# Decay steps on a ring of three banks, with the pairs on either side run among the steps

## What is computed

```
proj = h @ W_in.T;  gate, h_BC, dt = split(proj)          # 4096, 4096+2*128, 64 columns
h_BC = silu(conv over 4 taps of h_BC)                      # hidden, B, C
dt = softplus(dt + dt_bias);  At = -exp(A_log) * dt        # 64 heads, chunks of 32 tokens
L = exp(segment sums of At within a chunk)                 # [head, chunk, 32, 32]
y = ((C B^T * L) @ (hidden*dt) + chunk states) + D*hidden
x = x + ga * ((rmsnorm(y * silu(gate)) * norm_w) @ W_out.T)
```

## Time and profile before

| | us |
|---|---|
| median of 3 runs | 1593.89 |
| lowest and highest | 1591.78, 1598.0 |
| the profiled execution: its own time | 1599.31 |
| its span, first to last instruction | 1597.2 |
| mean granted TensorE clock | 0.949 of full |
| a transition, from yt of pair 31 to yt of the next batch's pair 0: three of them | 39.38, 40.16, 41.57 |
| the first batch's steps on DVE | 48.16 to 64.38 |

### The profile page before, as it was taken

How to read it: one execution, slowest core, us unless ns; L and a number is a source line. 1 busy time by engine, 2 the same in 40 slices (tenths; PEclk the granted TensorE clock), 3 DMA queues, 4 the chain that set the end, 5 groups by cost and what they waited for, 6 DMA issues and landing times.

```text
span 1597.2 us, 29712 instructions
## 1 busy us (share of the span) xinstructions
PE 1466.8 (92%) x9736; PEld 1143.2 (72%) x9736; DVE 1269.4 (79%) x2138; ACT 966.6 (61%) x1729; POOL 654.2 (41%) x554
## 2 busy tenths in 40 slices
PE   6799999799999789999879999877699999999979
PEld 5666666666766666666576676545598998998979
DVE  2788888698899788989779889943568988998954
ACT  3665666566566566656375656542267888887840
POOL 0134344133447524435814344834024544454530
PEclk7899999999999999999999999977769999999989
DMA  5376567466667755667847667713168989998858
GB/s 189 130 220 218 195 209 242 130 227 209 214 220 249 231 184 195 222 207 240 265 139 232 219 204 233 253 39 108 38 185 282 298 288 300 297 299 276 255 195 268
DMA packets 239686, 343.55 MB, mean 215 GB/s; under 512 B 20761, under 2 KB 191399, under 8 KB 238512
## 3 DMA queue, kind: packets, MB, share of 16 engines
q1 hardware_dynamic: 226096, 299.48, 59.4%
q0 software_dynamic: 13440, 42.19, 7.3%
HBM read 177.65 MB, written 172.30 MB: 219 GB/s over the span
## 4 chain that ended last, share of the span: by engine, by line
PE 64%; DVE 16%; issue 7%; ACT 5%; SPq 3%; DMA 2%; another core or an unknown queue 2%; POOL 1%; DVEq 0%; ACTq 0%; POOLq 0%
PE bank L451 12%; PE bank L618 11%; PE bank L453 10%; PE bank L452 10%; PE bank L629 6%; DVE e L1144 4%; PE bank L817 3%; PE bank L605 3%; DVE m L1185 2%; PE bank L793 2%; ACT e L880 2%; PE bank L763 2%; DVE e L1181 1%; DVE ew_lo L1077 1%
## 5 line engine op out<-in xcount | busy, mean ns | idle before, releaser
L1542 POOL TENSOR_TENSOR ssq<-ssq,ysq 128x512 f32<-128x512 f32 x128 | 167.8, 1311 | 428.7 <-ACT ysq L951 427.2
L1144 DVE SCALAR_TENSOR_TENSOR e<-bank,scal,e 128x511 f32<-128x511 f32 (+2 forms) x384 | 286.2, 745 | 35.2 <-ACT e L946 26.2
L1625 POOL DMA_INDIRECT outputs<-hsw,x_rows x160 | 181.6, 1135 | 238.0 <-DVE hsw L1488 185.7
L451 PE MATMUL bank<-h_hi,wi_hi 128*128 128x512 f32 x512 | 229.8, 449 | 33.2 <-issue 15.1
L618 PE MATMUL bank<-e,wn 128*128 128x512 f32 x512 | 247.6, 607 | 12.3 <-DVE e L1181 12.3
L1529 POOL TENSOR_TENSOR wi_lo<-wi,wi_hi 128x512 fp32r<-128x512 f32 x128 | 164.8, 1288 | 107.8 <-ACT wi_hi L828 107.8
L452 PE MATMUL bank<-h_lo,wi_hi 128*128 128x512 f32 x512 | 206.5, 403 | 0.0
L453 PE MATMUL bank<-h_hi,wi_lo 128*128 128x512 f32 x512 | 206.4, 403 | 0.0
L946 ACT ACTIVATE e<-bank,scal 128x512 f32<-128x512 f32 x128 | 99.4, 777 | 165.0 <-PE bank L453 163.4
L959 ACT ACTIVATE e<-e 128x512 f32<-128x512 f32 x128 | 80.7, 630 | 170.6 <-DVE e L1144 170.0
L1077 DVE TENSOR_TENSOR ew_lo<-ew,ew_hi 128x864 fp32r<-128x864 f32 x160 | 168.5, 1053 | 14.8 <-ACT ew_hi L828 8.1
(11 more groups left out here) (232 smaller groups left out, 3444.5 us busy)
## 6 DMA issues: line engine op xcount, KB each, us to landing
grouped<-zeros_out SPq DMA_DIRECT2D x256, 520.0 KB
ew<-expert_w SPq DMA_DIRECT2D x160, 432.0 KB
wi<-in_w SPq DMA_DIRECT2D x128, 256.0 KB
x_rows<-grouped SPq DMA_DIRECT2D x160, 130.0 KB
wo<-out_w SPq DMA_DIRECT2D x128, 128.0 KB
got<-outputs SPq DMA_DIRECT2D x16, 768.0 KB, 4.3
seg_wb<-seg_const POOLq DMA_DIRECT2D x4, 2048.0 KB, 8.3
seg_wa<-seg_const POOLq DMA_DIRECT2D x4, 2048.0 KB
```

The costliest lines, as they stand in the source:

```text
L451: mm(out, w_hi, x_hi, start=first, stop=False)
L1144: v.scalar_tensor_tensor(dst[:, d:], src[:, 0:SEQ - d], taps(TAPS - 1 - d), dst[:, d:], ALU.mult, ALU.add).then_inc(S[done], 1)
L1542: g_.tensor_tensor(ssq[:, :], ssq[:, :], ysq[:, :], ALU.add).then_inc(S["ssq_done"], 1)
L1625: g_.indirect_dma_start(outputs, bass.IndirectOffsetOnAxis(x_rows[:, i % XD, EMB:EMB + 1].bitcast(U32), 0), y_rows[:, i % YD, :], None, bo ...
```

## The change

1. The steps use a ring of three: banks 6, 2 and 3, and three buffers laid over `m` (two halves) and `xt` (`seg_e`). PE and ACT wait for the step three back in place of eight. PE waits before step 1 for the last `xt`, before step 2 for the last `y_skip`, and ACT before steps 0 to 2 for the last small matmuls (`ssm`).
2. Slot 33 of the old batch (output product, square of y) runs among the next batch's steps: at step 3 on PE and ACT, ahead of step 0 on DVE as before.
3. Sums of squares at step 5, their reading on DVE at step 8, copy out of p_out at step 6.
4. The next batch's pair 0: weights taken in during slot 31 of the old batch, hidden product at step 6, first tap at step 8, taps on DVE at step 10, gate product at step 10. Pair 1's weights are rounded at step 13 and its hidden product runs at step 26. C B^T runs at step 14, its mask at step 18. Both silus of pair 0 stay behind step 31.
5. Batch 0: its pair 0's weights are taken in at step 3; C B^T, its silu and its mask stay behind step 31; PE now waits before step 0 for all 6 taps of B and C (before, ahead of step 6).
6. SP loads the next batch's first two pairs in the loop's last two rounds; POOL starts the second half of the constants behind slot 31 and waits for three of the four send counters.

```diff
-SEG_BANKS = (6, 0, 1, 2, 3, 7, 4, 5)
+SEG_RING, SEG_BANKS = 3, (6, 2, 3)
+SEG_OUT, SEG_SUMS, SEG_HID, SEG_GATHER, SEG_TAP0, SEG_SQUARE, SEG_TAPS, SEG_GATE = 3, 5, 6, 6, 8, 8, 10, 10
+SEG_NEXT_IN, SEG_G, SEG_MASK, SEG_NEXT_HID = 13, 14, 18, 26
...
+            seg_e = (m[:, 0:2, :, :].rearrange("p t h l -> p (t h l)"), m[:, 2:4, :, :].rearrange("p t h l -> p (t h l)"),
+                     xt[:, :, :].rearrange("p t l -> p (t l)"))
...
-                if u >= RING:
-                    pe.wait_ge(S["seg_exp"], n - RING + 1)
+                if u == 1:
+                    pe.wait_ge(S["xt_done"], START["xt_done"] + b * PAIRS)
+                if u == 2:
+                    pe.wait_ge(S["y_skip"], START["y_skip"] + b * PAIRS)
+                if u >= SEG_RING:
+                    pe.wait_ge(S["seg_exp"], n - SEG_RING + 1)
...
+                pe.wait_ge(S["bc_taps"], 2 * (TAPS - 1) * (b + 1))
...
                 for u in range(CHUNK):
+                    if u == SEG_OUT and b:
+                        slot(b - 1, PAIRS + 1, 1, do_hid=False, do_in=False, do_mid=False, do_out="last")
+                        beside(b - 1, PAIRS + 1)
+                    if u == SEG_SUMS and b:
+                        pe.wait_ge(S["xhat"], (BATCH if b == 1 else BATCH + b - 1) * KE)
+                        square_sums(b - 1)
+                    if u == SEG_HID:
+                        hidden(b, 0, 0)
+                    if u == SEG_GATE:
+                        gating(b, 0, 0)
+                    if u == SEG_G and b:
+                        state_products(b)
+                    if u == SEG_NEXT_HID:
+                        hidden(b, 1, 1)
+                    segment(b, u)
+                if b == 0:
+                    state_products(b)
                 beside(b, 0)
-                slot(b, 1, 1, do_out="")
+                pe.wait_ge(S["seg_exp"], (b + 1) * CHUNK)
+                slot(b, 1, 1, do_hid=False, do_out="")
...
# ACT
-                if u >= RING:
-                    act.wait_ge(S["seg_done"], n - RING + 1)
+                if u >= SEG_RING:
+                    act.wait_ge(S["seg_done"], n - SEG_RING + 1)
+                else:
+                    act.wait_ge(S["ssm"], START["ssm"] + b * PAIRS)
...
+                    if u == SEG_OUT:
+                        if b:
+                            slot(b - 1, PAIRS + 1, 1, do_tap=False, do_in=False, next_in=False, take_out=False)
+                            beside(b - 1, PAIRS + 1)
+                        else:
+                            take_in(b, 0, 0)
+                    if u == SEG_GATHER and b:
+                        gather_out(b - 1)
+                    if u == SEG_TAP0:
+                        first_tap(b, 0, 0)
+                    if u == SEG_NEXT_IN:
+                        take_in(b, 1, 1)
                     segment(b, u)
...
# DVE
-                    if u == 5 and b:
+                    if u == SEG_SQUARE and b:
                         mean_square(b - 1)
+                    if u == SEG_TAPS:
+                        slot(b, 0, 0, do_mid=False, finish=False)
+                    if u == SEG_MASK and b:
+                        mask(b)
                     segment(b, u)
...
# POOL
-                    for t in range(HD):
+                    for t in range(3):
                         pool.wait_ge(S[f"sent{t}"], 16 * TOP_K * max(0, b - 1))
...
-                    slot(b, j, j % 2, next_in=j < PAIRS - 1, finish=j > 1)
+                    slot(b, j, j % 2, next_in=j < PAIRS - 1 or j == PAIRS - 1 and b + 1 < BATCH, finish=j > 1)
...
-                if b + 1 < BATCH:
-                    load_segments(b + 1, 1)
+                    if j == SECOND_SEGMENTS_AT and b + 1 < BATCH:
+                        load_segments(b + 1, 1)
```

More of the change, by code:

```diff
@@ L64 @@
 SHARE_AT = 25
-SEGMENTS_AT = 28
+SEGMENTS_AT, SECOND_SEGMENTS_AT = 28, 31
 GAP = 27
@@ L376, in _ @@
             for b in range(BATCH):
-                for par in range(2):
-                    load_in(b, par, par)
+                if b == 0:
+                    for par in range(2):
+                        load_in(b, par, par)
                 for j in range(PAIRS):
@@ L607, in slot @@
                 if do_in:
-                    pe.wait_ge(S["silu_g"], START["silu_g"] + g)
-                    for k in range(KE):
-                        w = slice(k * P, (k + 1) * P)
-                        i = split_mm(p_gate[:, :], wi_hi[:, par, w], wi_lo[:, par, w], h_hi[:, k, x], h_lo[:, k, x],
-                                     k == 0, k == KE - 1)
-                    i.then_inc(S["gate"], 1)
+                    gating(b, j, par)
                 if do_out:
@@ L654, in _, with state_products @@
             dt_turn(0)
[L655 to L679 removed]
+            def state_products(b):
+                pe.wait_ge(S["attn_scaled"], b * KE)
                 pe.wait_ge(S["bc_silu"], 2 * b + 2)
@@ L1196, in slot, with mask @@
                     dve.wait_ge(S["tap0"], g + 1)
-                    tap(1, acc[:, par, :], p_hid, lambda n: col(j, TAP_AT + n), "taps", (TAPS - 1) * g)
-                if do_in:
-                    for d in range(2, TAPS):
+                    for d in range(1, TAPS):
                         tap(d, acc[:, par, :], p_hid, lambda n: col(j, TAP_AT + n), "taps", (TAPS - 1) * g)
+            def mask(b):
+                dve.wait_ge(S["g_mm"], b + 1)
+                for hd in range(2):
+                    v.tensor_tensor(gmask[:, :, hd, :], p_out[0][:, :].rearrange("p (t l) -> p t l", t=TILES),
+                                    same[:, None, :].broadcast_to([P, TILES, P]), ALU.mult).then_inc(S["g_done"], 1)
             route = [0]
@@ L1374, in _ @@
                 for u in range(CHUNK):
-                    if u == 5 and b:
+                    if u == SEG_SQUARE and b:
                         mean_square(b - 1)
+                    if u == SEG_TAPS:
+                        slot(b, 0, 0, do_mid=False, finish=False)
+                    if u == SEG_MASK and b:
+                        mask(b)
                     segment(b, u)
+                if b == 0:
+                    mask(b)
                 dve.wait_ge(S["seg_done"], (b + 1) * CHUNK)
-                slot(b, 0, 0, do_mid=False, finish=False)
-                dve.wait_ge(S["g_mm"], b + 1)
-                for hd in range(2):
-                    v.tensor_tensor(gmask[:, :, hd, :], p_out[0][:, :].rearrange("p (t l) -> p t l", t=TILES),
-                                    same[:, None, :].broadcast_to([P, TILES, P]), ALU.mult).then_inc(S["g_done"], 1)
                 dve.wait_ge(S["g_done"], 2 * (b + 1))
```

120 lines of the change are left out of this document (55 added, 65 removed).

## The result

| | before, us | after, us |
|---|---|---|
| median of 8 runs each | 1592.68 | 1603.60 |
| lowest and highest | 1589.16, 1598.0 | 1598.96, 1608.01 |
| the profiled execution, its span | 1599.31, 1597.2 | 1601.5, 1599.4 |
| first step on DVE | 48.16 | 53.15 |
| from that step to the first yt | 31.09 | 35.51 |

After stands to before as 1.0054, 95% interval 1.0032 to 1.0077: the change makes the kernel 0.54% slower. 1580 us had been forecast, with a range of 1571 to 1593. Later, on another chip, the ratio was 1.0018 (0.999 to 1.0045).

What follows compares the result with a forecast made beforehand. PE was taken as the bound in the slots, with about 9 us idle per transition. Transitions -16.8 and batch 0 +2.7 gave -14.1 us off the median 1593.89: 1580 us, range 1571 to 1593 (8 in 10).

Steps and rivals of the forecast that it cites:

- these are the covers: Among a transition's steps: PE's 10.3 us of steps and 3.85 of moved products hide under 14.9 on DVE, costing nothing.
- The transitions, forecast 34.0, 34.8 and 35.6: From yt of pair 31 to yt of next pair 0: gains of 5.4, 5.4 and 6.0 us, in all 16.8.
- the late sum: Second transition: POOL's weights and constants' DMA ahead of the last sends put the last sum of squares about 0.8 us later.
- Batch 0, forecast +2.7 with bounds 0 and 5: First yt at 81.9 against 79.25: 2.7 us lost, 0 to 5 by whether the clock is low when PE starts.
- The wait in batch 0: Step 0 waits for the taps of B and C, ending at 48.24; DVE's step 6 then starts at 56.7.
- 6.9 us from last step to yt: End of a transition: table loads, silus, square root, pair 1's taps, reciprocal and diagonal put yt 6.9 us after the steps.
- The ring by itself: In the steps: three buffers cost nothing, as hand-over loops of 0.45 and 0.44 us stay under DVE's 0.52; bounds 0 to 10.
- The moved DMAs at nothing: New DMA orders on SP and POOL cost nothing; POOL's wait behind slot 31 bounded at 0 to 1.3 us, taken as 0.
- The two pauses of over 3 us go away: Argument against the clock falling: PE's two long transition pauses vanish, replaced by waits on banks of tenths of a us.
- The ends of batches, forecast nothing: Last slots of a batch: the change touches no slot from 2 to 31, so no cost there.
- What is put in does not hide: Rival: moved work costs in full, 5.6 us a transition and 3.4 in batch 0, 20.2 in all: 1600; chance 0.21.
- The clock falls during the steps: Rival: PE's small bank waits hold the clock at half, 14.7 us a transition, 54 in all; at half 1607; chance 0.09.

Runs made afterwards that it cites:

- ring4: After with batch 0 in before's order, plus a fourth bank and `yt` as fourth buffer, sums and slot 0's side work moved; median 1564.44 us, ratio 0.9995 to before.
- late_pair1: late_in with all of pair 1 (weights, hidden product) behind step 31 for batches 1 to 3; median 1577.59 us, ratio 0.9923 to before.
- after_fill0: After with the 8 dense matmuls that nothing reads also behind the first expert tile; median 1566.90 us, ratio 0.9987 to before.
- after_short: After with 16 expert tiles in place of 160 and the last sums fed from expert weights; median 1230.57 us.
- late_seg: late_in with the constants' DMA back behind slot 33, waiting for all four send counters; median 1583.80 us, ratio 0.9965 to before.
- late_in: After with batch 0 in before's order, and the next pair 0's weights taken in at step 3, not in slot 31; median 1562.17 us, ratio 0.9994 to before.
- fill: After with batch 0 in before's order, plus 6, 4 and 10 unread matmuls in PE's three pauses of a transition; median 1563.90 us, ratio 0.9993 to before.
- before_again: Before, unchanged, run once more for a second profile; 1564.37 us (one run), where before's median on that chip was 1565.03.

## Why the prediction was wrong

Wrong was the sign: forecast -14.1 us, measured +4 to +11. By the ledger the transitions gained 8.9 us in place of 16.8, batch 0 lost 9.8 in place of 2.7, and the ends lost 3.1 in place of nothing. The step that failed is the overlap: "these are the covers", by which what is put among the steps costs nothing beside DVE's own pace. Step by step:

- **The transitions, forecast 34.0, 34.8 and 35.6.** This is the largest miss, 7.9 us over three. At full clock one takes 36.2 to 36.3, and 37.1 with the late sum. "These are the covers, and they are thin" was right, and the first transition's sum failed by 2.3: 0.4 ahead of the taps, 1.1 where POOL's work lies beside a step, 0.9 behind pair 1's hidden product. ring4 gave back the wait and late_pair1 both. POOL's share stood nowhere in the sum. Half clock ahead of the taps adds 1.5 to 1.8; the forecast had 1.6 for it in the third transition only, and after had it in all three.
- **Batch 0, forecast +2.7 with bounds 0 and 5, measured 8.0 in the shown pair and 9.8 over four.** It came out over its own upper bound. Take the later head (1.4) off, and yt came at 87.3 where 81.9 was forecast. 0.8 was lost by step 6, since PE's first steps ran at half clock behind their 6.95 us of rest. 3.2 were lost among the steps: 1.1 in DVE's 1.71 us step beside POOL, 1.1 behind pair 1's hidden product, and the rest where PE ran at half clock behind its pause of 2.29 us; after_fill0 and after_short, without that half clock, end their steps 1.4 earlier. And 1.4 were lost behind the steps: the silu ended 0.2 later than forecast, and C B^T, behind a rest of PE of 3.30 us, ran at half and took 2.05 instead of 1.05. The timeline of PE of after:

```profile
80.53 2.05 PE L682 MATMUL bank<-bcf 128*128 128x128 f32 x8 [3.30 <-ACT bcf L898]
```

- **The wait in batch 0 was priced, the company wasn't.** The sum put DVE's step 6 at 56.7, where before's stands at about 51.2 by the earlier trace rows, 5.5 later; taking the wait away gave back 5.2 (51.25 to 46.06). The sum then let the moved work win half of this back. It did not: the old order, with the work behind the steps, gave 4.6 more.
- **The parts that held.** The order of events, the 3 us wait ahead of step 5 that goes away, the taps behind step 9, 6.9 us from last step to yt (6.96), the 0.8 for the late sum (0.9, where it came). The ring by itself at nothing: it costs 0 to 0.5 a transition. It isn't free once work lies among the steps, where a fourth buffer takes away 1.1. The moved DMAs at nothing: late_seg, with the constants' DMA at its old place, was 0.4 slower to the end of the taps and not faster.
- **"The two pauses of over 3 us go away".** One did. The other stays, 3.23 us behind the steps.
- **The ends of batches, forecast nothing.** +1.6 each: 0.5 from POOL's work beside DVE's comparison; the rest is clock, which isn't shown to come from the change. The forecast said that the change touches no slot from 2 to 31, which was false by its own list: pair 0's weights are taken in during slot 31.
- **The rivals.** "What is put in does not hide" is the nearest: it gave 5.6 a transition and 3.4 in batch 0 in full, and 1600 us. That this is near the measured 1603.6 is luck in part: the transitions missed by 2.3 of the 5.6 at full clock, and batch 0 by 5.4, more than its 3.4. "The clock falls during the steps" happened in small: 3.4 to 6.8 us per transition in most profiles, but never for the steps' whole length. Among the steps it fell behind pauses of 1.0 to 2.3 us; from the taps to the last step of a transition, where waits on the three banks were tenths of a us and at most 1.5, it stayed full in every profile of after's order.

## What to carry to other kernels

When work is moved into a stretch, price the first pass through the loop by itself: one wait that is free in the steady state cost 5 us once, more than one transition gave back. List for each moved GpSimd instruction what VectorE does beside it: 1.3 us of GpSimd was up to 1.1 us on VectorE's path. Compare the length of what is put among steps with the depth of their ring: a hidden product of 1.4 us made DVE wait 0.9 us on three buffers and not at all on four. Running the pairs' products in the slots around the steps, where PE is dense anyway, gained three times as much in the transition, and gave back 1.3 us in the last slots of a batch and 1.3 to 3.6 in its first 24 pairs.

## What the hardware did that was not expected

The clock can stay at half under full load. Some 95 us behind the last yt (in four profiles 111 to 115), at the start of the expert tiles and in late_in and fill behind PE pauses of 1.50 and 0.81 us, the clock falls, in some profiles for 3.4 us and in others for 27 to 31 (in two for 7 and 10). Here are 12 us stretches of late_in and of fill at the same place of the program, busy time by stretch; first late_in:

```profile
1127.80:1139.80 12.00, 11.81 (x118) 11.11 (x117) 11.63 (x24) 10.59 (x23) 5.67 (x5) 1.00 0.73 216
```

and fill:

```profile
1130.30:1142.30 12.00, 12.00 (x69) 12.00 (x68) 7.96 (x16) 7.18 (x15) 3.42 (x3) 0.50 0.71 203
1142.30:1154.30 12.00, 12.00 (x64) 11.61 (x63) 7.83 (x14) 6.11 (x13) 3.83 (x4) 0.50 0.68 207
```

PE is busy for 12.00 of 12.00 us and stays at 0.50; it comes back when the 8 dense matmuls of 512 columns behind tile 7 run. Behind the last yt four whole kernels with 3.4 us of it took 517.1 to 520.4 us, and seven with 27 to 31 took 525.5 to 529.0; late_in and fill differ by 11.1. That fits the two groups in before's times, 1556 to 1560 and 1563 to 1575 on one chip, where before_again, the one profile of before, has the long stretch and 1564.4 us; the lower group has no profile. The same matmuls behind the first tile made before 0.5% faster (before_fill0) with nothing else changed.

Chips differ by more than the change: before's median was 1592.7, 1565.0, 1566.5, 1566.6, 1571.5 and 1591.2 us in six sets of runs. And the start, up to PE's first matmul, took between 7.1 and 12.3 us from execution to execution.
